# Four scan banks and two for the rest: a fused patch-token, scan and FFN kernel on one Trainium2 core

## The reference, cut to what matters

```
h = patch_tokens(x); h = concat([h, txt], axis=1)
# scan over every second token of layernorm(h), state (256 x 64) per picture
x_proj, gate = split(rmsnorm(layernorm(h)[:, ::2]) @ w_in.T + b_in)
h_t = tanh(h_{t-1} * A + x_t[:, :, None] * Bm)
y_t = h_t @ Cm.sum(0) + Dv * x_t
h = h + repeat((y * silu(gate)) @ w_out.T + b_out, 2)
f = layernorm(h)
out = h + (silu(f @ wg.T) * (f @ wu.T)) @ wd.T
```

## Time and profile before

| | |
|---|---|
| median of 3 runs | 1422.66 us (1420.58 to 1423.19) |
| the profiled execution | 1424.49 us |
| its span | 1422.6 us |
| mean granted TensorE clock | 0.963 |
| busy: PE, DVE, ACT, POOL | 88%, 76%, 71%, 31% of the span |

### The profile page before, as it was taken

The page is one execution under the profiler, slowest core; times in us unless marked ns, Lnnn a source line. Parts: engine busy times, 40 slices in busy tenths (PEclk is TensorE's granted clock), DMA queues, the critical chain, the costliest instruction groups (busy, mean ns, idle before and its releaser), DMA issues.

```text
span 1422.6 us, 25915 instructions
## 1 busy us (share of the span) xinstructions
PE 1248.4 (88%) x7199; PEld 642.3 (45%) x7199; DVE 1079.0 (76%) x2401; ACT 1010.4 (71%) x1955; POOL 439.5 (31%) x443
## 2 busy tenths in 40 slices
PE   3858899999999999999999999999889989988865
PEld 1623345454545454545444445454344444433333
DVE  4638788888878787878787878787888888878621
ACT  1446786868686868787878786877877778768612
POOL 5303152515161615242424343423212122121121
PEclk8769999999999999999999999999999999999987
DMA  7230414141414142332324141303232232231210
GB/s 184 65 66 19 112 29 115 32 112 33 109 33 109 45 97 62 80 78 64 88 54 104 38 111 31 98 7 108 56 89 72 55 105 56 65 81 53 53 52 7
DMA packets 154926, 100.52 MB, mean 71 GB/s; under 512 B 129088, under 2 KB 143296, under 8 KB 153536
## 3 DMA queue, kind: packets, MB, share of 16 engines
q1 hardware_dynamic: 154880, 99.95, 28.1%
HBM read 58.85 MB, written 41.06 MB: 70 GB/s over the span
## 4 chain that ended last, share of the span: by engine, by line
PE 36%; issue 22%; ACT 12%; DVE 9%; DMA 8%; POOL 6%; SPq 3%; ACTq 0%; DVEq 0%; POOLq 0%
PE U L1114 7%; PE Y L1124 7%; DVE U L693 5%; ACT h L881 4%; PE P L1259 4%; DMA y_scr<-y_fx 4%; PE P L1260 4%; PE P L1199 3%; PE P L1168 3%; PE P L1274 2%; PE P L1275 2%; DMA yT<-y_scr 2%; POOL raw_s L1006 2%; DVE act L810 2%; SPq L582 1%
## 5 line engine op out<-in xcount | busy, mean ns | idle before, releaser
L693 DVE TENSOR_TENSOR U<-h,a_col 128x512 f32<-128x512 f32 x1096 | 722.6, 690 | 182.4 <-ACT h L881 175.9
L881 ACT ACTIVATE h<-U 128x512 f32<-128x512 f32 x1096 | 626.9, 598 | 221.3 <-PE U L1114 216.8
L1114 PE MATMUL U<-x_diag,b_st 128*128 128x512 f16 x1096 | 389.8, 387 | 80.7 <-DVE U L693 68.3
L1124 PE MATMUL Y<-h,read_st 128*32 128x512 f32 x2192 | 296.5, 613 | 0.3 <-ACT h L881 0.3
L1114 PEld LDWEIGHTS U<-x_diag,b_st 128*128 128x128 f16 x1096 | 104.9, 99 | 336.3 <-DVE U L693 275.8
L1056 POOL TENSOR_TENSOR xT_act<-act,xT_act 128x448 f16<-128x448 f32 x120 | 127.7, 1071 | 196.8 <-ACT xT_act L965 196.7
L1168 PE MATMUL P<-tok_w,xT_act 128*112 128x256 f32 x672 | 171.1, 387 | 1.6 <-ACT xT_act L898 1.6
L1168 PEld LDWEIGHTS P<-tok_w,xT_act 128*112 128x112 f32 x672 | 117.8, 179 | 53.5 <-issue 21.8
L1274 PE MATMUL P<-down_w,xT_act 128*112 128x256 bf16 x480 | 114.9, 277 | 4.9 <-POOL xT_act L1056 4.9
L1275 PE MATMUL P<-down_w,xT_act 128*112 128x256 bf16 x480 | 113.7, 275 | 0.0
L810 DVE SCALAR_TENSOR_TENSOR act<-fsg,P 128x448 f32<-128x448 f32 x120 | 73.9, 615 | 41.0 <-PE P L1260 28.4
(11 more groups left out here) (136 smaller groups left out, 1485.7 us busy)
## 6 DMA issues: line engine op xcount, KB each, us to landing
raw<-in_x SPq DMA_DIRECT2D x42, 448.0 KB, 6.2
tok_scr<-tok SPq DMA_DIRECT2D x20, 448.0 KB, 3.3
gate_scr<-gate_o SPq DMA_DIRECT2D x20, 448.0 KB, 2.5
gate_fx<-gate_scr SPq DMA_DIRECT2D x20, 448.0 KB, 5.3
res<-tok_scr SPq DMA_DIRECT2D x20, 448.0 KB, 3.6
out<-res SPq DMA_DIRECT2D x76, 112.0 KB, 2.3
x_diag<-scan_scr SPq DMA_DIRECT2D x320, 16.0 KB
x_diag<-scan_scr SPq DMA_DIRECT2D x304, 12.0 KB
```

Source lines behind the costliest of these rows:

```text
L693: dve.tensor_tensor(U[bank_of(slot)][:, :].rearrange("p (l b) -> p l b", b=B), h[:, c, :].rearrange("p (l b) -> p l b", b=B), a_col[:, c * ...
L881: sc.activation(h[:, c, :], U[bank_of(slot)][:, :], ACT.Tanh, scale=1.0 / U_SCALE).then_inc(squashed, 1)
L1114: pe.matmul(U[bank_of(slot)][:, :], b_st[:, c, :], x_diag[:, c, :, t * B:t * B + B], start=False, stop=True, skip_group_check=True).then_i ...
L1124: mm = pe.matmul(Y[c4 * 32:c4 * 32 + 32, :], read_st[:, t, half, :], h[:, half * RG + c4, :], start=(j == 0), stop=(t == steps - 1), skip_ ...
```

## The change

- `NU` is 4 and there are two P banks. `turn` alternates P[0] and P[1]; `embed` uses P[1] and P[0]; `turn_xa` and `project` use P[1]; `turn_fx` P[0] and P[1]. In image bodies `turn_xa` waits for the FFN's product 0 and the two projections for products 1 and 3, and the up products behind them wait for their copies.
- h is a ring of 14 chunks: `squash` writes chunk slot % 14, `grow` reads chunk (slot - 8) % 14. `read_step` reads eight chunks at once, at slots 3, 11, 19, ... (READ_AT = 3).
- The bias of attend is one bf16 product of ones [96 x 112] with a row split into three bf16 parts at partitions 0, 32 and 64, over both halves (512 columns). The parts are made in the setup by 11 VectorE instructions (2 memsets, 9 of one row).
- The gate is loaded into a tile of its own, `gate_in`, and SP issues that load ahead of the wait for y.
- All entries of `PLANS` and `POOL_ORDER` are new. For the image body `turn` goes from slots 7 to 14 to slots 7 to 13, `attend` from 16, 16 to 15, 15, the FFN's first gate product from 36 to 33, `turn_xa` from 40 to 36, `project` from 43, 43, 47, 55 to 40, 40, 47, 47, `y_copy` from 1 to 0. For the text body `ln_stats` goes from 19 to 22, `project` from 24, 25, 34, 43 to 28, 28, 29, 32.
- The DMA scratch reserved for the program is 4096 bytes in place of 8192.

```diff
-READ_AT = 2
-NU = 3
+READ_AT = 3
+RING = 14
+NU = 4
+XA_AFTER, X_AFTER, GATE_AFTER = 1, 2, 4
...
-                                  h[:, c, :].rearrange("p (l b) -> p l b", b=B),
+                                  h[:, (slot - CHUNKS) % RING, :].rearrange("p (l b) -> p l b", b=B),
...
-            def read_group(j, s, steps):
...
+            def read_step(t, s, steps):
+
+                pe.wait_ge(squashed, s * SLOTS + (t + 1) * CHUNKS)
+                if t == 0 and due(s):
+                    pe.wait_ge(y_out, s)
+                for half in range(CHUNKS // RG):
+                    for c4 in range(RG):
+                        mm = pe.matmul(Y[c4 * 32:c4 * 32 + 32, :], read_st[:, t, half, :],
+                                       h[:, (t * CHUNKS + half * RG + c4) % RING, :], start=(t == 0 and half == 0),
+                                       stop=(t == steps - 1 and half == CHUNKS // RG - 1), skip_group_check=True)
...
         def turn_bank(n):
-            return (2, 1, 0)[n % 3]
+            return n % 2
...
-                if n >= 3:
-                    pe.wait_ge(xT_done, g * 8 + n - 2)
+                if n >= 2:
+                    pe.wait_ge(xT_done, g * 8 + n - 1)
...
                 elif post:
-                    pe.wait_ge(fxT_done, (q + 1) * 4)
+                    pe.wait_ge(act_done, q * HB + XA_AFTER)
...
+                if image and post:
+                    pe.wait_ge(act_done, q * HB + (X_AFTER, GATE_AFTER)[part])
...
+                if k == 0:
+                    pe.matmul(P[0][0:PT, 0:2 * D], bias_one[:, :], bias_row[:, :].unsqueeze(1).to_broadcast([BIASP, 2, D]),
+                              start=True, stop=False, skip_group_check=True)
...
                 if k > 0 and which == 1:
                     pe.wait_ge(act_done, q * HB + k)
+                    if pre and image and k == XA_AFTER:
+                        pe.wait_ge(xaT_done, g + 1)
+                    if pre and image and k == X_AFTER:
+                        pe.wait_ge(xf_done, (g + 1) * 2)
+                    if pre and image and k == GATE_AFTER:
+                        pe.wait_ge(gf_done, (g + 1) * 2)
...
+                sp.wait_ge(gate_wr, (q + 1) * 16)
+                sp.sem_inc(passed, 1)
+                if due(q):
+                    sp.wait_ge(z_done, q)
+                    sp.sem_inc(passed, 1)
+                sp.dma_start(gate_in[:, :].rearrange("p (a n) -> p a n", a=2), gate_scr[q]).then_inc(gate_ld, 16)
                 sp.wait_ge(y_out, q + 1)
```

More of the change, by code:

```diff
@@ L63 @@
     "image": dict(
-        shrink=(0, 0, 0, 1, 2, 4, 4, 6), turn=(7, 9, 9, 10, 13, 13, 14, 14), attend=(16, 16), average=(23, 27),
-        embed=(17, 18, 20, 21, 21, 24, 25, 26, 27, 28, 28, 32), turn_fx=(29, 32), ffn_gate=(36, 37, 45, 46, 48, 51),
-        ffn_up=(36, 39, 45, 47, 51, 53), turn_xa=(40,), project=(43, 43, 47, 55), finish=(6, 9), raw_patch=(10, 10,
-        10, 11, 13, 14, 16, 16, 16, 16, 16, 17, 17, 17), raw_means=(18,), raw_deviation=(27,), raw_variance=(31,),
-        res_stats=(21,), res_variance=(23,), res_shift=(27,), fx_low_part=(32, 36), tok_stats=(28, 34),
@@ L86 @@
+        ffn_up=(44, 50, 52, 54, 55, 55), finish=(11, 19), res_stats=(32,), res_variance=(37,), res_shift=(45,),
+        fx_low_part=(46, 54), ffn_product=(55, 55, 55, 55, 55, 55), y_copy=(5,), fx_apply=(38, 38, 38, 38),
+        fxT_copy=(42, 49), ffn_silu=(50, 54, 55, 55, 55, 55), act_high_part=(51, 54, 55, 55, 55, 55), residual=(30,)),
     "first": dict(
-        turn=(0, 2, 2, 2, 2, 2, 2, 2), average=(19, 23), embed=(4, 6, 6, 6, 7, 7, 7, 8, 8, 8, 9, 9), turn_xa=(32,),
-        project=(36, 37, 39, 43), raw_patch=(1, 2, 2, 2, 2, 3, 3, 3, 3, 8, 8, 16, 16, 18), raw_means=(20,),
@@ L94 @@
[L94 to L100 removed]
+        turn=(4, 4, 4, 6, 6, 6, 7, 7), average=(32, 43), embed=(7, 7, 8, 8, 8, 8, 8, 8, 14, 20, 22, 31),
@@ new lines @@
+        ffn_even=(20, 26, 26, 26, 32, 35), ffn_odd=(48, 55, 55, 55, 55)),
+    "second": dict(
+        turn=(0, 0, 0, 0, 0, 0, 0, 2), average=(14, 16), embed=(5, 8, 9, 12, 12, 17, 17, 18, 20, 24, 24, 29),
+        turn_xa=(34,), project=(37, 40, 45, 45), raw_patch=(6, 7, 7, 9, 10, 11, 11, 13, 13, 13, 15, 16, 16, 16),
+        raw_means=(16,), raw_deviation=(17,), raw_variance=(17,), tok_stats=(19, 35), tok_shift=(20, 36),
+        ln_stats=(27,), ln_shift=(31,), raw_shift=(27,), x_low_part=(44,), xT_copy=(0, 0, 0, 0, 0, 0, 0, 3),
+        tok_normalise=(19, 35), ln_apply=(31,), xaT_copy=(32,), x_copy=(40,), gate_silu=(51,), normalise=(50, 51,
+        55, 55, 55, 55, 55)),
@@ L1133, in average @@
                         pe.wait_ge(res_done, q + 1)
+                    elif pre and scan:
+                        pe.wait_ge(xT_done, g * 8 + 7)
+                    elif pre:
+                        pe.wait_ge(tok_small, g * 16 + 10)
                     src = raw_mv[:, :, 0]
@@ L1223, in turn_fx @@
                     pe.wait_ge(res_done, q + 1)
-                    if ahead:
-                        pe.wait_ge(raw_small, r * 6 + 5)
+                    if pre and image:
+                        pe.wait_ge(tok_small, g * 16 + 10)
                 elif pre and image:
@@ L1240, in ffn @@
                     pe.wait_ge(fx_lo_done, (q + 1) * 2)
-                if k == 0 and which == 1:
-                    if pre and image:
-                        pe.wait_ge(tok_small, g * 16 + 10)
-                    elif down:
-                        pe.wait_ge(out_done, d * 2 + 2)
                 if k > 0 and which == 0:
```

192 lines of the change are left out of this document (100 added, 92 removed).

## The result

The changed kernel takes 1437.7 us (median of 4 runs, 1436.02 to 1446.82), the kernel before 1421.65 us (median of 4); the ratio is 1.0123, 95% interval 1.0098 to 1.0149. The forecast was 1369 us with a range of 1328 to 1430: it was wrong, in direction too. The profiled execution took 1436.02 us, its span is 1434.2 us, 11.6 us above that of before (the medians are 16 us apart).

What follows compares the result with a forecast made beforehand. PE was taken as the fullest engine, though not alone, with DVE full in some image slots. Image groups -32.5 us, text -15.5 and -4.5, scan's end -1, tail -1.3, setup +1: -54 us, to 1369 us, range 1328 to 1430.

Steps and rivals of the forecast that it cites:

- Queues and orders: SP's gate load ahead of the wait for y, and plan moves: gate load -2 us, in the tail only.
- bank terms of the image groups: Per image group: fourth scan bank -2.9 us, only two banks for all other products +2.2 us.
- PE's work: TensorE work in either kind of group falls by 1.8 us through longer reads and the bf16 bias.
- The bias: Attend's bias as one bf16 product replaces four passes a group: -0.64 us of PE, setup +1 us.
- The reads: Reads of eight: a 2.01 us visit replaces two of 1.09 us, seven times a group, -1.2 us of PE.
- two bank terms: Per text group: fourth scan bank -3.8 us, two banks for other products, through three hand-offs in a row, +2.5 us.
- Waits shorter than 0.6 us vanish, longer ones shrink by 0.6: How the fourth scan bank shortens PE's waits for a grow: 2.9 us per image group, 3.8 us per text group.
- rival 4: P[1] hand-offs and turns exposed at their upper bound, 6.8 us an image group: 1430 us; chance 0.15.
- rival 3: The 2.0 us read eats the lead the fourth bank gives, ACT waiting behind each read: 1429 us; chance 0.08.
- four rivals: Two banks free, 1326 us (0.11); DVE full, 1407 (0.16); long read, 1429 (0.08); hand-offs exposed, 1430 (0.15).
- The sign given for the forecast: Marks of a right forecast, among them drives waiting for grows for about 1 us a group.
- The sentence on the clock: Clock shares of the long middle are 1.00, the 2.4 GHz level, so no part of the sum rests on it.

Runs made afterwards that it cites:

- run 1: Changed kernel with the gate load issued behind y's writes again, its own tile kept: 1416.8 us, ratio 0.9976.
- run 2: Kernel before with only the gate load changed, into its own tile and ahead of the wait for y: 1442.7 us, ratio 1.0165.
- run 6: Changed kernel with the gate load behind y's writes and the image body's residual moved from slot 19 to 21, its statistics 20 to 22: 1404.7 us, ratio 0.9901.
- run 8: Kernel before with the bias as one bf16 product alone: 1409.4 us, ratio 0.9925.
- run 14: Changed kernel with three scan banks and three other banks: 1561.4 us, against 1569.9 us with three scan banks and two others.
- run 15: Changed kernel, gate load behind y's writes, residual two slots later, a_col in SBUF, its bank a third other bank: 1523.1 us; control with two other banks 1530.9 us.
- run 9: Changed kernel with reads four at a time, behind drives 3 and 7 of each eight, all else kept: 1471.7 us, ratio 1.0343.

## Why the prediction was wrong

**The step that failed is the gate load in "Queues and orders".** "The gate load's waits are long over when it is reached, so nothing new is held up behind it" is true of semaphores and false of bytes: 448 KB went ahead of y's four writes, the reads of yT came 0.9 us later into a group than in the kernel before though y was issued earlier, 1.3 us later than in run 1, and the reload of the residual, last in that chain, reached DVE in the stretch where it is full. I costed this at 0 in the image groups and at -2 us in the tail. It was +21 us (run 1) and +22.7 us (run 2), and 0 in the tail. This step decides the sign: without it the changed kernel takes 1416.8 us. It is not the largest part of the miss of 69 us; that is in the bank terms of the image groups, below, off by 2.4 us a group.

**A step that was missing: the residual moved from slot 20 to 19**, one slot earlier, while its load came later. I listed the plans' moves and did not hold each against the landing of what it reads. The wait is 26.4 us over nine groups, and two slots later are worth another 12 us (run 6 against run 1), most of it by the clock. These two make 33 us; the changed kernel without them is faster than the one before, by 0.99%.

**PE's work was right in kind and too small**: -2.25 us a group against -1.8. The bias gave 0.65 as forecast. The reads gave 1.6 in place of 1.2: a visit of eight adds 1.95 us between two drives where I had 2.01, against two visits of 1.09 us.

**The text part was right in its time, and by luck.** A text group takes 53.15 us against 52.8, and 2.25 of the 2.75 us won are PE's work, so that the two bank terms, -3.8 and +2.5 in the forecast, came to -0.5 together. Neither was right by itself. PE's waits for a grow went from 3.6 us to 2.9 us, here from 1108.4 to 1161.5 us, where I had expected about 1 us:

```profile
PE U L1134 <- DVE U L714: 2.9, 10, 0.7
```

PE's wait for ACT at the hand-offs is 0.7 us there and was 0.6 us before, so the +2.5 us did not come either. These are readings of one group each and no experiment; run 8 shows for the kernel before that less work of PE need not shorten a text group at all.

**The image bank terms were wrong by sign.** -2.9 and +2.2 were to give -0.7. In run 6, with the chain of y mended, PE's idle time in an image group is 9.3 us where it was 7.6: +1.7. The step that failed is "Waits shorter than 0.6 us vanish, longer ones shrink by 0.6". PE's waits from 286 to 970 us, before and then in run 6:

```profile
PE U L1114 <- DVE U L693: 26.7, 57, 1.2
```

```profile
PE U L1134 <- DVE U L714: 30.8, 49, 1.5
PE P L1189 <- ACT xT_act L918: 7.1, 10, 0.8
PE P L1296 <- DVE fx_split L836: 6.8, 10, 0.8
PE P L1219 <- ACT xa L932: 3.4, 9, 0.4
```

The drives wait fewer times for a grow, but as long in all, about 3 us a group: under the new plan the fourth bank took nothing off this sum, where I had counted on 2.9 us. Of the other three lines, only the wait for the FFN's low part stood among those of before, with 0.2 us in all. The turns (0.7 us a group) and `turn_xa` (0.4 us) are hand-offs, and with the 0.7 us for fx_split they add up to about the +1.7 us. This is read from two traces, and no run tests it line by line.

The two banks' hand-offs, rival 4, are the small part: to have two banks and not three cost 8.5 us in all (run 14) and 8 us (run 15) where I had about 44 us (2.2 in 13 and 2.5 in 6 groups), and nothing in a steady image group. Both pairs stand on kernels that other losses had slowed, so in the changed kernel itself this cost is not measured. Nor did rival 3 come true with four banks (run 9). The longest of the waits for a grow is in slot 33 of the new plan, in the changed kernel here from 690 us (PE, then DVE and one line of POOL):

```profile
691.74 0.99 PE L1269 MATMUL P<-cst,y_fx 112*128 112x112 f32 x8
694.22 0.39 PE L1134 MATMUL U<-x_diag,b_st 128*128 128x512 f16 x1 [1.49 <-DVE U L714]
695.28 0.36 PE L1296 MATMUL P<-fx_split,gate_w 128*128 128x448 f16 x1 [0.67 <-DVE fx_split L836]
695.48 0.47 PE L1297 MATMUL P<-fx_split,gate_w 128*128 128x448 f16 x1
695.74 0.58 PE L1296 MATMUL P<-fx_split,gate_w 128*128 128x448 f16 x1
696.11 0.58 PE L1297 MATMUL P<-fx_split,gate_w 128*128 128x448 f16 x1
```

```profile
690.93 0.76 DVE L756 TENSOR_TENSOR tok<-P,rows 112x256 f32<-112x256 f32 x2 [0.62 <-PE P L1202]
691.60 0.74 DVE L760 BATCH_NORM_STATS2 tok_st<-tok 112x6 f32<-112x256 f32 x2
692.49 0.25 DVE L764 BATCH_NORM_AGGREGATE tok_mv<-tok_st 112x2 f32<-112x6 f32 x2
692.77 0.79 DVE L766 TENSOR_SCALAR tok_s<-tok_mv 112x2 f32<-112x2 f32 x1
693.48 0.68 DVE L714 TENSOR_TENSOR U<-h,a_col 128x512 f32<-128x512 f32 x1
...
692.27 1.27 POOL L1071 TENSOR_TENSOR tok<-tok,rows 112x512 f32<-112x512 f32 x1
```

Slot 32's token statistics wait 0.6 us for the embed products of slot 28, then hold DVE for 2.6 us, and the next grow is late: PE stands 1.5 us and then 0.7 us more for fx_split. The same two gaps stand in run 6. The kernel before has a gap at the same work too, only shorter:

```profile
605.79 0.17 DVE L745 TENSOR_SCALAR tok_s<-tok_mv 112x2 f32<-112x2 f32 x1
...
606.64 0.39 PE L1114 MATMUL U<-x_diag,b_st 128*128 128x512 f16 x1 [1.15 <-DVE U L693]
```

The small L766 takes 0.79 us in the changed kernel and ends with POOL's L1071, which runs beside it (692.27 to 693.54 us); before, all 28 records of the same instruction, L745, are 0.17 us. So part of the longer gap seems to come with the new order on POOL, which the prediction did not look at. No run moves the statistics or POOL's product.

**The sum, mended.** From run 6, whose span is 19.3 us below that of before, to the forecast's 54 us there are some 35 us missing: 25.4 in the image groups (-0.4 a group on average where -2.5 was forecast, twelve times), 4.3 in the text groups (-2.2 against -3.1, five times), 2.5 at the start and 2.3 at the end.

**On chances.** The cause that decided was in none of the four rivals. Rival 4 reached the right side for a wrong reason, and its own sign is small, as the waits above show; its time of 1430 us is itself the upper bound of the range that was to leave it out. The sign given for the forecast, drives that wait for a grow about 1 us a group, did not come either. The sentence on the clock failed as well: the image part was granted 0.97 in place of 1.00.

## What to carry to other kernels

Moving a transfer past a wait is not free when the wait is over: count the bytes that then stand ahead of the small transfer on which the chain hangs, and follow that chain to the last of its loads and to the slot that reads it. When a plan is new, hold every entry that moved earlier against the landing of its operand; two slots were worth 12 us here, and reads one slot off their plan 68 to 90 us. Price a bank by taking it away under the plan that uses it, and expect the answer to hold for that plan alone: with other plans the three-bank kernel was 1421 us, and with these 1570.

## What the runs showed of the hardware

**DVE with two SBUF inputs and POOL hold each other up.** With a_col in PSUM, grows took 672 to 697 ns in the 338 records from 560 to 970 us. With a_col in SBUF the median was 693 ns (690 before) but the longest took 1769, and POOL's normalise rose from 557 to 996 ns on average. The PSUM bank of a_col pays for itself: 126 us. The Trainium skill, "SBUF — State Buffer", SBUF: two separate sides, says that a VectorE operation with two SBUF inputs and a GpSimd operation that reads SBUF take one port pair in turn, each for its whole length; the runs agree. By the Trainium skill, "Perfetto Trace Analysis", Optimizing Scalar/DVE Operations, which gives VectorE a smaller access overhead on SBUF than on PSUM, the move would have been a small gain; the shortest grow is 671 ns where it was 672.

**The clock fell after short gaps, and not after all of them.** Behind the 1.49 and 0.67 us that PE stood in slot 33, the products of L1296 and L1297 follow each other at 0.37 us in place of 0.19, and the windows show the lower level:

```profile
694.00:695.60 1.60, 0.71 (x3) 0.31 (x4) 1.60 (x4) 1.60 (x4) 0.00 (x0) 1.00 0.00 0
695.80:697.00 1.20, 1.20 (x5) 0.48 (x4) 1.20 (x4) 0.00 (x0) 0.00 (x0) 0.50 0.00 0
697.00:700.00 3.00, 3.00 (x18) 0.94 (x20) 2.63 (x9) 1.96 (x4) 2.24 (x2) 0.67 0.00 0
```

0.50 is the 1.2 GHz level. Of nine steady image groups of the changed kernel each has such a stretch. Five have it behind slot 33 and take 71.0 to 71.4 us. Three have it at the wait for zT, of 2.4 us, and take 72.3 us, as the group from 576.9 us on, where the granted clock is 0.50 from 596.6 to 603.4 us; they keep the full clock behind slot 33. The ninth has a short one just behind the wait for zT.

In run 6 the gaps of slot 33 stand as well, PE waits 0.9 us for zT, and no steady image group falls to the lower level. In run 1 PE waits as long for zT and has the same gaps, and seven of nine groups do fall. So these gaps do not settle it, and what does is not shown. Where the clock fell, a wait was paid twice, once as the wait and once as slower products behind it.
